# A two-layer network on 8 batches: the work around the second attention placed beside its score steps, scores kept in DRAM, query tiles in the order 0, 1, 2, 3

## The reference, cut to what matters

```python
x = layernorm(x + attn0(x))      # 16 heads of 8, rope, causal softmax, x: 8 x 512 x 128, float32
x = layernorm(x + ffn0(x))       # silu(x@w1)*(x@w2), gelu(h1), gelu(h2), w3; hidden 512
x = layernorm(x + attn1(x))      # below
x = layernorm(x + experts(x))    # top 4 of 16 experts of 64, plus one shared expert

# attn1, for each of 8 batches; 16 heads of 64, 4 memory keys ahead of 512 keys
q, k = l2norm(x @ Wq), l2norm([mem_k, x @ Wk]);  v = [mem_v, x @ Wv]
dots = 10 * einsum('bhid,bhjd->bhij', q, k)
dots = einsum('hg,bgij->bhij', W_pre_th, dots)          # mixes the heads
dots = where(causal, -max, dots)
dots = where(dots < top_k(dots, 64)[..., -1:], -max, dots)
attn = einsum('hg,bgij->bhij', W_post_th, softmax(dots))  # mixes them again
out = einsum('bhij,bhjd->bhid', attn, v) * head_scale * sigmoid(x @ Wg + bg) @ Wo
```

## Time and profile before

| | us |
|---|---|
| median of 3 runs | 4687.48 (4676.58 to 4687.7) |
| the profiled execution's own time | 4677.0 |
| its span, first to last instruction | 4675.4 |
| PE, DVE, ACT, POOL busy, share of the span | 69%, 56%, 44%, 30% |
| mean granted TensorE clock | 0.782 of 2.4 GHz |
| first block of a batch to that of the next (2381.3 to 2954.7) | 573.4 |

### The profile page before, as it was taken

One profiled execution on the slowest core, in us unless ns is written; L12 is line 12 of the kernel. 1 busy time (PEld: TensorE's weight loads), 2 busy tenths in 40 slices (PEclk: granted clock), 3 DMA queues, 4 the chain that ended last, 5 costly groups with the idle time before them and its releaser, 6 DMA issues. The chain is left out here.

```text
span 4675.4 us, 63627 instructions
## 1 busy us (share of the span) xinstructions
PE 3245.3 (69%) x19124; PEld 1917.1 (41%) x19124; DVE 2600.1 (56%) x9042; ACT 2074.2 (44%) x5898; POOL 1379.7 (30%) x3919
## 2 busy tenths in 40 slices
PE   3777567675786757767667776687766777667766
PEld 1345423453334532345323453235532355323543
DVE  2367743666436664466643775437753477534774
ACT  1356413664226642266322763227622376124770
POOL 1035501354013540145301453014520145102551
PEclk6877778777687777977778777787787877778787
DMA  2021210212102120022200221002210112101111
GB/s 89 1 37 24 47 47 0 40 27 52 36 0 41 29 53 32 0 43 30 51 29 7 40 33 46 29 15 33 32 45 29 20 29 31 45 29 28 23 30 48
DMA packets 99769, 151.99 MB, mean 33 GB/s; under 512 B 19518, under 2 KB 86998, under 8 KB 96126
## 3 DMA queue, kind: packets, MB, share of 16 engines
q1 hardware_dynamic: 99326, 146.87, 15.4%
HBM read 64.90 MB, written 9.59 MB: 16 GB/s over the span
## 5 line engine op out<-in xcount | busy, mean ns | idle before, releaser
L666 PE MATMUL pm<-mixin,pre_b 128*128 128x258 f32 (+15 forms) x1088 | 466.7, 552 | 343.0 <-ACT xs L790 160.6
L505 POOL TENSOR_TENSOR rstd<-var,powers 128x4 f32<-128x4 f32 x32 | 32.5, 1015 | 1623.3 <-DVE var L515 1623.3
L679 PE MATMUL pt<-wsc,attn 128*128 128x128 f32 x2560 | 445.2, 333 | 87.0 <-POOL wsc L574 86.3
L614 PE MATMUL pa<-kT,qT 64*128 64x132 f32 (+3 forms) x1024 | 327.2, 533 | 239.8 <-ACT dots L772 128.7
L679 PEld LDWEIGHTS pt<-wsc,attn 128*128 128x128 f32 x2560 | 391.6, 236 | 168.5 <-POOL wsc L574 123.7
L799 ACT ACTIVATE ex<-xs,thr 128x420 f32<-128x420 f32 (+12 forms) x624 | 347.6, 560 | 179.2 <-POOL thr L591 149.6
L666 PEld LDWEIGHTS pm<-mixin,pre_b 128*128 128x128 f32 x1088 | 216.4, 244 | 478.4 <-issue 321.7
L1084 DVE TENSOR_REDUCE dots<-po 128x1 f32<-128x384 f32 (+3 forms) x374 | 222.9, 638 | 339.8 <-PE po L1070 339.8
L857 DVE MAX8 top<-xs 128x8 f32<-128x420 f32 (+15 forms) x384 | 163.5, 434 | 441.3 <-ACT xs L790 440.4
L589 POOL TENSOR_SCALAR shift<-signs 128x2 f32<-128x2 f32 x624 | 127.6, 205 | 677.7 <-ACT ex L799 340.7
L772 ACT ACTIVATE dots<-pa,rq 128x388 f32<-128x388 f32 (+3 forms) x512 | 228.0, 473 | 208.9 <-PE pa L614 169.9
(11 more groups left out here) (261 smaller groups left out, 7613.7 us busy)
## 6 DMA issues: line engine op xcount, KB each, us to landing
dots<-moe_dram SPq DMA_DIRECT2D x8, 2176.0 KB, 9.2
kT<-parts_dram SPq DMA_DIRECT2D x216, 64.0 KB
dots<-ffn_dram SPq DMA_DIRECT2D x8, 1536.0 KB, 6.8
at<-ffn_dram SPq DMA_DIRECT2D x8, 1280.0 KB, 10.7
mixin<-dots SPq DMA_DIRECT2D x32, 258.0 KB
mixin<-dots SPq DMA_DIRECT2D x32, 242.0 KB
mixin<-dots SPq DMA_DIRECT2D x32, 226.0 KB
parts_dram<-at SPq DMA_DIRECT2D x18, 384.0 KB, 4.0
```

The source lines that it names most:

```text
L614: nc.tensor.matmul(bank_of(("qk", t, 2 * c + odd, z))[:, 0:jn], qT_v[at:at + HD1, c, P * t:P * t + P], kT_v[at:at + HD1, c, j0:j0 + jn], s ...
L666: ins = nc.tensor.matmul(bank[:, 0:jn], pre_b[:, :], mixin[:, m % MIX_SLOTS, j0:j0 + jn], start=True, stop=not last)
L679: ins = nc.tensor.matmul(bank[:, P * k:P * k + P], attn[:, m % A_SLOTS, P * k:P * k + P], wsc[:, m % A_SLOTS], start=True, stop=True)
```

## The change

The loop's turn becomes one block, `period(b)`. It runs the score steps of batch b, and beside them the experts of batch b-1 and everything of batch b+1 up to its scores. An `opening` block does the latter for batch 0 alone, in sequence; a `closing` block does the experts of batch 7. In the last period the front part runs on padding.

- `schedule()` gives each side item a slot. A step s from -1 to 38 has four slots, 4s to 4s+3; the items lie in slots -5 to 125, that is in steps -1 to 31. All five streams call `beside(slot)` at four fixed places of each step (the loop over s in the diff is ACT's). The item `s` is one of 22 pairs of row maxima, `st` two heads of the first attention's scores, `values0` its product with the values, `f`, `h1`, `h2` the first feed-forward part, `m` and `cb` the experts' products.
- The scores of a batch go to DRAM (`dots_scratch`, two halves, one per parity of the batch): 32 items `qk`, two heads each, ACT scales them into one of four `fresh` slots, and SP writes them out (`dots`). `scores_sync` loads `mixin` from there.
- `TILE_ORDER` is 0, 1, 2, 3; `ahead(s)` only makes values and gates now. The side items use the banks `pa` and `po` together with the steps. The first attention's scores use both `pa` banks in place of `pa` and `pm`, and one buffer of exponentials in place of two.
- The SBUF tensors of the side work lie in one area `side` of 18112 columns; `xs`, `ex` and `left` get buffers of their own. At the head of a period POOL copies `x2` and `xe` from the side area.
- The norm of the query lengths is computed transposed (32 small products in place of 8 and 4 transposes), and the experts' pads are full width.

```diff
-TILE_ORDER = (3, 1, 0, 2)
+TILE_ORDER = (0, 1, 2, 3)
+def schedule():
...
+    put(-5, "moe")
+    put(-5, "norm", 0, "a")
+    put(-5, "ones")
+    put(-5, "zero")
...
+    one_by_one((-2, 0, 1, 3), [("parts", 0), ("parts", 1), ("stack", 0), ("stack", 1)])
+    one_by_one((0, 2, 4, 5, 7), [("x3T",), ("lg",), ("gexp",), ("gating",), ("cT",)])
+    for k in range(MC + 1):
+        put(8 + k, "m", k)
+        if k:
+            put(8 + k, "cb", k - 1)
+    for n in range(len(S_PAIRS)):
...
+        put(12 + n, "s", n)
...
+    one_by_one((24, 35), [("rows", g) for g in range(SETS)])
+    one_by_one((21, 23, 25), [("norm", 1, "a"), ("norm", 1, "b"), ("out",)])
+    products = (35, 39, 41, 43, 48, 51, 53, 55)
+    heads = ((31, 32, 33, 34), (35, 36, 37, 38), (39, 39, 40, 40), (41, 41, 42, 42),
+             (44, 45, 46, 47), (48, 49, 50, 50), (51, 51, 52, 52), (53, 53, 54, 54))
...
+    one_by_one((66, 67, 68, 69), [("f", k) for k in range(KC)])
+    one_by_one((70, 71, 72, 73), [("h1", k) for k in range(KC)])
+    one_by_one((78, 79, 80, 81), [("h2", k) for k in range(KC)])
...
+    one_by_one((92, 93, 94, 95), [("k", t) for t in range(TT)])
+    one_by_one((96, 96, 97, 97, 98, 98, 99, 99), [("q", k) for k in range(NC)])
+    one_by_one((102, 103, 103, 103, 104, 104), [("qs",), ("knorm",)] + [("kmul", t) for t in range(TT)])
+    one_by_one((105, 105, 106, 106, 107, 107, 108, 108), [("keys", k) for k in range(NC)])
+    for n in range(TT * NC):
+        put(109 + n // 2, "qk", n // NC, n % NC)
+        put(110 + n // 2, "dots", n // NC, n % NC)
...
+            for s in range(-1, END):
+                fresh_values, fresh_gates = ahead(s)
+                if 0 <= s < STEPS:
+                    mixed(s)
+                search = 1 <= s <= STEPS and searched(s - 1, plan)
+                if search:
+                    count(s - 1, 0)
+                if 4 <= s < STEPS + 4:
+                    posted(s - 4)
+                beside(4 * s)
+                for what in fresh_values:
+                    values(what[1])
+                beside(4 * s + 1)
+                if search:
+                    count(s - 1, 1)
+                if 2 <= s < STEPS + 2:
+                    exponentials(s - 2)
+                for what in fresh_gates:
+                    gates(what[1])
+                beside(4 * s + 2)
+                if search:
+                    count(s - 1, 2)
+                beside(4 * s + 3)
...
-                tile = dots[R8 * u:R8 * u + R8, SCORES_AT[t]:SCORES_AT[t] + H1 * wt].rearrange("p (g j) -> p g j", g=H1)
-                sp.dma_start(mixin[:, m % MIX_SLOTS, 0:wn], tile[:, :, 0:wn]).then_inc(mix_in[m % MIX_SLOTS], 16)
+                tile = dots_d[dots_in, ROWS_AT[t]:ROWS_AT[t + 1]].rearrange("(p j) -> p j", j=wt)
+                sp.dma_start(mixin[:, m % MIX_SLOTS, 0:wn], tile[P * u:P * u + P, 0:wn]).then_inc(mix_in[m % MIX_SLOTS], 16)
...
+            elif name == "dots":
+                o, k = rest
+                t, n = TILE_ORDER[o], NC * o + k
+                wt = MEM + P * (t + 1)
+                sp.wait_ge(a_free, A.nth(("qk", o, k, len(pieces(wt)) - 1, 1)))
+                tile = dots_d[dots_at, ROWS_AT[t]:ROWS_AT[t + 1]].rearrange("(q n) -> q n", q=P)
+                sp.dma_start(tile[:, 2 * k * wt:2 * (k + 1) * wt], fresh[:, n % D_SLOTS, 0:2 * wt]).then_inc(dots_out[n % D_SLOTS], 16)
...
         with nc.Block() as block:
-            start(block)
+            opening(block)
         clear_semaphores()
         with nc.Fori(0, B) as b:
             with nc.Block() as block:
-                front(block)
+                period(b, block)
             clear_semaphores()
...
-            with nc.Block() as block:
-                experts(b, block)
-            clear_semaphores()
+        with nc.Block() as block:
+            closing(block)
+        clear_semaphores()
```

More of the change, by code:

```diff
@@ L78, in narrow @@
     return n >= NARROW_FROM
[L81 to L101, removed]
@@ L109, with ahead, pair_of, has_tail @@
+BESIDE = schedule()
+LAST_SLOT = max(BESIDE)
+def ahead(s):
+    values = [("vx", s)] if 0 <= s <= TT else []
+    gates = [("g", t) for o, t in enumerate(TILE_ORDER) if s == STEPS_TILE * o + STEPS_TILE // 2 + 1]
+    return values, gates
+def pair_of(s):
+    return [(z, PAIR * s + z, SEQ[PAIR * s + z]) for z in range(PAIR)]
+def has_tail(s):
+    return SEQ[PAIR * s] % PER_TILE >= PER_TILE - GROUP
+def last_piece(n):
+    return len(pieces(width(n))) - 1
 class Ring:
@@ new lines, with __init__, beside, mine @@
+class Plan:
+    def __init__(self, scores, full=False, experts=False, front=False):
+        self.scores, self.full, self.experts, self.front = scores, full, experts, front
+        order = self.order()
+        a, o = ([x for what in order for x in banks_of(what)[z]] for z in range(2))
+        self.A, self.O = Ring(a), Ring(o)
+        self.M = Ring([("mix", m, z) for m in range(SUBS) for z in range(len(pieces(width(SEQ[m]))))])
+        self.T = Ring([("post", m) for m in range(SUBS)])
+        self.norms = ([0, 1] if experts else []) + ([2, 3] if front else [])
+    def beside(self, slot):
+        def mine(what):
+            expert = what[0] in EXPERT_ITEMS or what[0] == "norm" and what[1] < 2
+            return self.experts if expert else self.front
+        return [what for what in BESIDE.get(slot, []) if mine(what)]
+    def order(self):
+        out = self.beside(FIRST_SLOT)
+        if not self.scores:
+            for slot in range(FIRST_SLOT + 1, LAST_SLOT + 1):
+                out += self.beside(slot)
+            return out
+        for s in range(-1, END):
+            values, gates = ahead(s)
+            mixes = [("mix", m, n) for z, m, n in pair_of(s + 1)] if s + 1 < STEPS else []
+            posts = [("post", m, n) for z, m, n in pair_of(s - 3)] if 3 <= s < STEPS + 3 else []
+            late = [mixes.pop() for n in range(len(mixes)) if last_piece(mixes[-1][2])][::-1]
+            out += mixes[:1] + self.beside(4 * s) + values + mixes[1:] + self.beside(4 * s + 1) + gates
+            out += posts[:1] + self.beside(4 * s + 2) + posts[1:] + self.beside(4 * s + 3)
+            if posts and has_tail(s - 3):
+                out.append(("tail", s - 3))
+            if s >= STEPS_BLOCK + 3 and (s - 3) % STEPS_BLOCK == 0 and (s - 3) // STEPS_BLOCK <= S // RB:
+                out.append(("av", (s - 3) // STEPS_BLOCK - 1))
+            if s > STEPS_TILE and (s - 5) % STEPS_TILE == 0:
+                out.append(("wo", (s - 5) // STEPS_TILE - 1))
+            out += late
+        return out + ([] if self.full else [("bad",)])
@@ L195, in network @@
         mixin = sb("mixin", [P, MIX_SLOTS, J])
[L196 to L202, removed]
+        xs = sb("xs", [P, X_SLOTS, J])
+        ex = sb("ex", [P, E1_SLOTS, J])
+        left = sb("left", [P, PAIR, J])
         attn = sb("attn", [P, A_SLOTS, J])
@@ L1274, in _ @@
[L1274 to L1284 removed]
+                pe.wait_ge(x_in, 32)
@@ L1332, in _ @@
-                act.wait_ge(rq_done, 1)
-                scores_scalar(act, RINGS, False)
+                for slot in range(FIRST_SLOT, LAST_SLOT + 1):
+                    for what in OPENING.beside(slot):
+                        side_scalar(act, OPENING, what)
             @block.vector
@@ L1541, in _ @@
[L1541 to L1546 removed]
+                for slot in range(FIRST_SLOT, LAST_SLOT + 1):
+                    for what in CLOSING.beside(slot):
+                        side_vector(dve, chain, CLOSING, what)
```

1651 lines of the change are left out of this document (876 added, 775 removed).

## The result

The changed kernel takes 4827.9 us (median of 4 runs, 4822.8 to 4832.9) beside 4687.4 us of the kernel before: a ratio of 1.0305, 95% interval 1.0286 to 1.0325. It is slower; forecast were 4340 us and a range that ended at 4640. The profiled execution took 4824.4 us with a span of 4822.7.

What follows compares the result with a forecast made beforehand. Waiting between three sequential stages, no engine above 69% busy, was taken as most of what can be won. Opening 322, eight beats of 492 and closing 72 gave 4330, plus 10 for the median: 4340 us, range 4080 to 4640.

Steps and rivals of the forecast that it cites:

- The new beat is, step by step, the time of the busiest engine ... plus the ends that nothing covers: Each period: largest engine per step, main plus side work, 478 us, less 15, plus ends and stalls: beat 492 us.
- (c): Stalls of the new hand-overs in a period, at the 3% by which the method's check fell short: 13 us.
- the check on the old order: The same pricing applied to the old kernel's steps gave 288 us; the trace has 303, some 8 of it first-gather wait.
- the sheet: Every instruction priced by shape, main and side work summed per step, largest engine taken: 478 us a period.
- The gathers ... I take nothing: Score gathers from DRAM, issued two steps ahead, replace gathers that took 8 us to the first product; no cost added.
- rival 3: SP's queue: gathers stand behind its new waits, one in two late by 1.5 us; +24 a period, 4530 us; chance 0.12.
- `qk` at 2.2 ns a column: PE's price for the next batch's score products at mean clock 0.78; all 32 items, 20736 columns: +45 us in the opening.
- Steps 32 to 38 at 36 us, start 8, flag and barrier 8: Period's ends: last steps without side work 36 us, chained steps -1 to 1 8 us, flag, barrier and semaphore clearing 8 us.
- The opening: All front work for batch 0 in sequence before the first period, which was to start near 322 us.
- Rival 2: Hand-overs of `pa` and `po` set the beat: 0.48 us for each of some 275 fills, 556 us, 4850 in all; chance 0.14.
- Rival 1: The clock rises as PE gets fewer gaps: beat about 460 us, 4084 us in all; chance 0.20.
- Rival 4: No overlap in effect, one late item stopping all five streams: beat near 535, 4680 us, the same time; chance 0.04.

Runs made afterwards that it cites:

- experiment 8: Changed kernel with tile order 1, 2, 3, 0, one next-batch head pair a slot, stack transfers one to two steps later and gathers first: 4442.8 us, ratio 0.9476.
- (5): Changed kernel with both gathers of a step issued first and the stack's transfers one to two steps later: 4727.1 us, ratio 1.0089.
- (3): Changed kernel with one of the next batch's head pairs a slot in place of two: 4672.4 us, ratio 0.9973.
- (2): Changed kernel with the tiles in the order 1, 2, 3, 0: 4695.5 us, ratio 1.0022.
- experiment 10: Changed kernel with tile order 1, 2, 3, 0 and one next-batch head pair a slot, stack transfers and gathers not moved: 4583.6 us, ratio 0.9781.
- experiment 4: Changed kernel with all side work left out of the periods, every period reading batch 0's scores: 2625.5 us, ratio 0.561.
- Experiment 6: Changed kernel with the next batch's scores of tiles 0, 1 and 2 made in two halves, 48 more `pa` fills a period: 5084.0 us, ratio 1.0854.

## Why the prediction was wrong

- **The stages and the price of the work: right.** PE's busy time in a period is 400 us, forecast 408; DVE 313; ACT 275. PE stayed first. The method's sum of the work held. The change did shorten the beat, from 573.4 to 549.3; forecast were 81 us less a beat, and it is 24, less than the longer ends take back.
- **"The new beat is, step by step, the time of the busiest engine ... plus the ends that nothing covers": this step failed.** It gave 492 and the beat is 549.3. By tile, with borders at the first row maxima, forecast and measured: tile 0 with the start 118 and 136.5; tile 1 83 and 105; tile 2 112 and 104; tile 3 with all behind it 181 and 206.5. The forecast then took 15 off and added 13 for stalls. In PE's terms: 69 us more idle (153 for 84), 8 less busy. Tile 2 came out shorter than its sum, in a stretch where the clock was 0.91 and the price assumed 0.78.
- **The term behind it: (c), 13 us of stalls.** It was taken from the check on the old order, where the sheet gave 288 of 303 us; 8 of the 15 missing were the wait for the first gather, so the steps' own shortfall was 7. There the steps had no side work beside them but the scores of the later tiles. With side work in all of them PE waits for banks, gathers, copies and scaled matrices for some 139 us a beat, and the beat is 57 us over the sum that allowed 13. Three edits take 46.5 of these 57 back (experiment 8). Alone they gave 10.3 for SP's waits (5), 17.4 for two `qk` items a slot (3) and 18.8 for the widest tile at the end (2); experiment 10 shows that this division isn't unique. The other 11 a beat are left open. After the three edits PE still waits on `pa` and `po`, 12.8 us for ACT in the first attention alone; no run took these hand-overs away.
- **"The gathers ... I take nothing": wrong,** 20.5 us of waiting a beat. The price of rival 3 (24) was close; its cause was not a gather late by 1.5 us each, but one long stop behind POOL and the stack. Moving the stack gave 10.3 of them back.
- **`qk` at 2.2 ns a column: a little low.** The items busy PE for 47.1 us a period as forecast (45 to 47), and without them the beat falls by 54.7.
- **Steps 32 to 38 at 36 us, start 8, flag and barrier 8: too low** with tile 3 last, 74 from maxima to maxima where these make 52. Without any side work it is still 55 to 59 with tile 3 last (by the row maxima in experiment 4), so the sum was low even for the steps alone. With tile 0 last it is 52, a coincidence, since the sheet priced tile 3 there.
- **The opening: 49 us low.** The `qk` items were to take 45 us there. By the view of their line they start at 290.4, and the opening ends at 371.3: 81 us, 36 more. The window, and the products' group in it:

```profile
290.40:371.30 80.90, 63.83 (x164) 34.24 (x164) 2.84 (x12) 35.11 (x81) 2.28 (x3) 0.52 0.34 133
```

```profile
L854 PE MATMUL pa<-side 64*128 64x258 f32 (+3 forms) x160 | 61.6, 697 | 11.2 <-ACT side L963 11.2
```

The 80 products busy PE for 61.6 us where a period's take 47.1: the clock granted is 0.52, not the 0.78 of the price. 11.2 more are waits for ACT. The other 13 us of the 49 weren't divided.
- **Rival 2 forecast 4850 us,** 22 from the result. In part that is luck: its beat of 556 is 54 us too long over eight batches, its ends of 394 are 34 too short. Its own sign was PE idle for over 100 us a period on `pa` and `po`; there are 88, or 0.32 us for each of 275 fills, under the 0.40 from which it was to decide. The remaining distance came from gathers and from the end, which it didn't name. Experiment 6 speaks for a price of fills and against its mechanism, since of 0.62 us a fill only 0.07 was waiting; 0.27 was the product's own fixed time and most of the rest the clock. I count it half right.
- **Rival 1, the clock: no.** 0.763 in place of 0.782 before. **Rival 4** (4680) was 148 us off. Its picture, no overlap, fits only beside the dense stages of before; against the side work by itself the overlap was real (549 for 684, experiment 4).
- **Costed at nothing, table loads: right.** By ACT's groups the period's window has 16 of them at 1.28 us. Two are the start of this period and of the next (L1325, ahead of which ACT stands at the barrier), so a beat has 15; forecast were 14:

```profile
L1345 ACT ACT_TABLE_LOAD x7 | 9.0, 1283 | 0.1
L975 ACT ACT_TABLE_LOAD x3 | 3.8, 1283 | 0.1
L1325 ACT ACT_TABLE_LOAD x2 | 2.6, 1283 | 43.4 <-issue 43.4
L933 ACT ACT_TABLE_LOAD x1 | 1.3, 1283 | 0.0
```

Three more of one each are not shown. The Trainium skill (ScalarE: Activation LUTs, "What ACT_TABLE_LOAD costs") has about 2.66 us for a switch with its drain; this trace has 1.28 and, within the period, at most 0.1 us of idle time ahead of a line's loads. The writes of 516 KB of scores landed within the 2.2 to 4 us forecast:

```profile
dots_scratch<-side SPq DMA_DIRECT2D x72, 516.0 KB, 2.6
```

- **Two small slips of the sums.** In the example of step 29, 5696 columns at 2.2 ns are 12.5 us, not 12.2. The range's upper end, 4530 and 128 more, is 4658, not 4640. Neither touches the result. The slower case had a chance of 0.15 and was left out of the range.

## What to carry to other kernels

When two bodies of work are interleaved by hand in five in-order streams, the time of the busiest engine in each step, at the clock it is priced at, is only a lower bound. Allow for stalls from a part that already has both kinds of work beside each other, not from one that runs almost alone. Count the pipeline's filling and draining too: here they cost 337 us more than before over only 8 turns, and a beat 24 us shorter didn't pay for them. Then look for three things before giving the overlap up, which here turned 3% slower into 5% faster: what a DMA queue's wait holds up behind it, whether the added items bunch in a few steps, and which piece of work is the last to drain.

## What the runs showed of the hardware

- A narrow product has a fixed price. The view of stretches for the scores' products alone, in the opening, at a clock of 0.50 in both kernels: 16 products of 260 and 16 of 388 columns in the changed kernel, then the same columns as 32 of 130 and 32 of 194 in experiment 6. Two records are one product:

```profile
300.20:315.00 14.80, 12.68 (x32) 6.81 (x32) 0.50 0.36 136
315.10:334.10 19.00, 16.95 (x32) 7.66 (x32) 0.50 0.40 161
```

```profile
307.60:328.10 20.50, 17.00 (x64) 12.22 (x64) 0.50 0.26 98
328.20:353.00 24.80, 21.13 (x64) 12.95 (x64) 0.50 0.32 124
```

A record takes 0.40, 0.53, 0.27 and 0.33 us. Worked out from these four rows, that is an estimated 0.13 us and 1.0 ns a column, for float32 on 64 rows at this clock.
- The clock did not follow PE's busy share: 0.91 in the stretch from 2801.7 with PE busy for 81%, 0.68 in the one before it with 76%, 0.62 in experiment 6's last steps with 83%, 0.52 with 79% in the opening's end, where the scores' products stand alone. The share isn't independent of the clock, since the same products busy PE for longer at the lower one. What lowers it there (their 64 rows, their widths, the pauses between) was not tried apart. A faster arrangement of the same instructions also got a higher clock, 0.781 in experiment 8 beside 0.763, and 85 us less of PE's busy time came with it.
